# A ViT tower kernel's embedding: both units of every second double group multiplied in rounded parts

## The reference, cut to what matters

```python
xb = 2.0 * jnp.pi * xyz[..., None] * freq_bands            # 6 frequency bands
feat = jnp.concatenate([jnp.sin(xb), jnp.cos(xb)], axis=-1)
feat = feat.reshape(b, n, -1)                              # 4 x 512 x 6912
h = jnp.einsum('bnf,of->bno', feat, W)                     # -> 4 x 512 x 192
```

## Time and profile before

| | value |
|---|---|
| median of 3 runs | 993.34 us (992.94 to 995.34) |
| the profiled execution: its time | 992.54 us |
| its span, first to last instruction | 990.8 us |
| TensorE busy over the span | 896.9 us (91%) |
| VectorE busy over the span | 696.6 us (70%) |
| ScalarE busy over the span | 645.6 us (65%) |
| GpSimd busy over the span | 142.0 us (14%) |
| embedding, first to last matmul | 8.97 us to 288.87 us |
| images 0, 1, 2 (from first matmul to first matmul) | 72.69, 68.62, 68.99 us |

### The profile page before, as it was taken

The page is one execution under the profiler, slowest core; times in us unless marked ns, Lnnn a source line. Parts: engine busy times, 40 slices in busy tenths (PEclk is TensorE's granted clock), DMA queues, the critical chain, the costliest instruction groups (busy, mean ns, idle before and its releaser), DMA issues. The chain is left out here.

```text
span 990.8 us, 19970 instructions
## 1 busy us (share of the span) xinstructions
PE 896.9 (91%) x6459; PEld 794.4 (80%) x6459; DVE 696.6 (70%) x1643; ACT 645.6 (65%) x1218; POOL 142.0 (14%) x204
## 2 busy tenths in 40 slices
PE   6999999999988899989998999898699996699996
PEld 5999999999976677667767776676498875699995
DVE  6889859769633796488648864887556335687775
ACT  5767757649624797589758974987444331886862
POOL 1000000000000144114311441244300000000000
PEclk9999999999997899999999999999789997799997
DMA  8021101089812696169526952795300020443201
GB/s 275 23 71 51 44 27 37 21 125 149 128 34 70 185 293 174 51 210 298 160 58 205 297 156 62 216 294 138 107 1 1 18 87 24 119 164 97 72 2 64
DMA packets 83801, 114.11 MB, mean 115 GB/s; under 512 B 12271, under 2 KB 44476, under 8 KB 83724
## 3 DMA queue, kind: packets, MB, share of 16 engines
q1 hardware_dynamic: 82636, 112.39, 41.2%
q10 hardware_dynamic: 1088, 0.79, 0.2%
HBM read 62.31 MB, written 47.67 MB: 111 GB/s over the span
## 5 line engine op out<-in xcount | busy, mean ns | idle before, releaser
L417 PE MATMUL psum<-w,feat 128*128 128x192 f32 x912 | 160.4, 331 | 11.9 <-ACT feat L347 9.0
L417 PEld LDWEIGHTS psum<-w,feat 128*128 128x128 f32 x912 | 149.3, 192 | 12.8 <-issue 10.3
L646 POOL TENSOR_SCALAR a_scores<-a_scores,a_inv 112x514 f32<-112x514 f32 (+1 forms) x160 | 113.0, 707 | 268.1 <-DVE a_inv L1018 267.9
L1003 DVE CUSTOM_DVE_ANT_0 a_scores<-psum,a_bias 112x514 f32<-112x514 f32 (+1 forms) x160 | 110.0, 688 | 46.6 <-PE psum L722 38.2
L875 ACT ACTIVATE a_scores<-a_scores,a_least 112x514 f32<-112x514 f32 (+1 forms) x160 | 116.7, 729 | 9.8 <-DVE a_least L1003 9.1
L735 PE MATMUL psum<-ident,a_scores 112*112 112x112 f32 (+1 forms) x800 | 100.2, 256 | 18.1 <-DVE a_probsT L1013 10.8
L435 PE MATMUL psum<-w_parts,parts 128*128 128x384 f32 x368 | 113.7, 374 | 0.8 <-DVE parts L227 0.8
L347 ACT ACTIVATE feat<-turn 128x1024 f32<-128x1024 f32 (+1 forms) x60 | 58.4, 974 | 82.5 <-PE psum L437 43.4
L735 PEld LDWEIGHTS psum<-ident,a_scores 112*112 112x112 f32 (+1 forms) x800 | 75.3, 134 | 40.3 <-issue 19.4
L722 PE MATMUL psum<-a_kh,a_q 128*112 128x258 f32 (+1 forms) x320 | 99.6, 333 | 1.0 <-DVE a_least L1003 1.0
L437 PE MATMUL psum<-w_parts,parts 128*128 128x192 f32 x384 | 96.6, 252 | 0.0
(11 more groups left out here) (297 smaller groups left out, 1808.2 us busy)
## 6 DMA issues: line engine op xcount, KB each, us to landing
shear<-a_pos SPq DMA_DIRECT2D x128, 224.9 KB, 3.7
a_bias<-shear SPq DMA_DIRECT2D x128, 224.4 KB, 3.7
shear<-zero SPq DMA_DIRECT2D x20, 448.9 KB, 15.7
e_fc<-in_e_fc_dram SPq DMA_DIRECT2D x16, 384.0 KB, 3.9
x<-in_xT_dram SPq DMA_DIRECT2D x20, 256.0 KB, 3.0
e_proj<-in_e_proj_dram SPq DMA_DIRECT2D x8, 576.0 KB, 5.4
shear<-a_pos SPq DMA_DIRECT2D x32, 130.5 KB
a_bias<-shear SPq DMA_DIRECT2D x32, 130.3 KB
```

The lines of the kernel that those rows point to most:

```text
L417: mm = pe.matmul(sums[m][:, 0:D], feat[:, r, j, 0, 128 * m:128 * m + 128], w[:, k, :], start=begins, stop=ends)
L646: pool.tensor_scalar(row, row, inv[0:TILES[g % NT][1], g % TT:g % TT + 1], 1.0, ALU.mult, ALU.mult).then_inc(weighed, 1)
L1003: dve.tensor_tensor_reduce(halves(scores[0:r, g % TT, 0:PADL]), psum2(score_pair(g), r), halves(bias[0:r, g % MR, :]), -1.0 / 8, BIG, ALU. ...
```

## The change

`full` holds the odd double groups: 1, 3, 5, 7, 9 and 11. Of these the first unit, too, is multiplied in rounded parts; the other groups stay as they were. For each full group and image, ScalarE rounds one more `feat` block (128x1024, both sine and cosine of the unit), VectorE takes one more difference (128x1024), and TensorE runs a second `split` in place of `native`. In the first image there is for each full group one more rounding of weights on ScalarE and one more difference of weights on VectorE. VectorE writes the differences, of both units and of every double group, over the unrounded features in `feat` itself, through a second tensor of type fp32r at the same address (`over`), so that the new array `high` holds only rounded values and has the size of the old `parts`. The raw weights of the full groups arrive by the same transfers as before, into the place in which their difference will stand. The reserved scratch for dynamic DMA is set to 1024 bytes.

```diff
+    full = [g for g in pairs if g % 2 == 1]
+    NFULL = len(full)
+    before = lambda g: sum(e < g for e in full)
+    native_units = [g for g in range(NE) if g not in full]
...
+        def over(n, sh):
+
+            with nc.sbuf_tensor(n, sh, F32) as plain:
+                pass
+            return plain, sb(f"{n}_parts", sh, F32R)
+
         x = sb("x", [128, 5, N])
-        w = sb("w", [128, 2 * NE, D])
+        w_native = sb("w_native", [128, len(native_units), 2, D])
+        w_place, w_first = over("w_first", [128, NFULL, 2, 2, D])
+        first_raw = lambda g: w_place[:, before(g), :, 1, :]
         raw = s.place.rearrange("p (g j n) -> p g j n", g=NPAIR, j=2)
-        feat = sb("feat", [128, NF, 2, 2, N])
+        feat, feat_place = over("feat", [128, NF, 2, 2, N])
         w_parts = sb("w_parts", [128, NPAIR, 2, 2, D], F32R)
-        parts = sb("parts", [128, NF, 2, 2, N], F32R)
+        high = sb("high", [128, NF, 2, 2, N], F32R)
...
-                sp.dma_start(w[:, 2 * g:2 * g + 2, :], s.d["tok_wT"][k0:k0 + 2].rearrange("k p n -> p k n")).then_inc(w_in[g], 16)
+                first = first_raw(g) if g in full else w_native[:, native_units.index(g)]
+                sp.dma_start(first, s.d["tok_wT"][k0:k0 + 2].rearrange("k p n -> p k n")).then_inc(w_in[g], 16)
...
             def rest(b, g):
                 r = g % NF
                 dve.wait_ge(hi_done, b * NPAIR + g + 1)
-                dve.tensor_tensor(parts[:, r, 1], feat[:, r, :, 1, :], parts[:, r, 0].bitcast(F32), ALU.subtract).then_inc(lo_done, 1)
+                dve.tensor_tensor(feat_place[:, r, :, 1, :], feat[:, r, :, 1, :], high[:, r, :, 1, :].bitcast(F32), ALU.subtract).then_inc(lo_done, 1)
+
+            def split_first_weights(g):
+                dve.wait_ge(first_w_hi, before(g) + 1)
+                dve.tensor_tensor(w_first[:, before(g), :, 1, :], first_raw(g), w_first[:, before(g), :, 0, :].bitcast(F32),
+                                  ALU.subtract).then_inc(first_w_lo, 1)
+
+            def first_rest(b, g):
+                r = g % NF
+                dve.wait_ge(first_hi, b * NFULL + before(g) + 1)
+                dve.tensor_tensor(feat_place[:, r, :, 0, :], feat[:, r, :, 0, :], high[:, r, :, 0, :].bitcast(F32), ALU.subtract).then_inc(first_lo, 1)
...
                     absolute(b, g)
+                    if first and g - 1 in full:
+                        split_first_weights(g - 1)
+                    if g - 1 in full:
+                        first_rest(b, g - 1)
                     if g - 1 in pairs:
                         rest(b, g - 1)
...
+            def split_first_weights(g):
+                act.wait_ge(w_in[g], 16)
+                act.copy(w_first[:, before(g), :, 0, :], first_raw(g)).then_inc(first_w_hi, 1)
+
             def first_parts(b, g):
                 r = g % NF
                 act.wait_ge(sin_done, b * NE + g + 1)
                 act.wait_ge(cos_done, b * NE + g + 1)
-                act.copy(parts[:, r, 0], feat[:, r, :, 1, :]).then_inc(hi_done, 1)
+                if g in full:
+                    act.copy(high[:, r, :, 0, :], feat[:, r, :, 0, :]).then_inc(first_hi, 1)
+                act.copy(high[:, r, :, 1, :], feat[:, r, :, 1, :]).then_inc(hi_done, 1)
...
                 group(0, g, True)
+                if g in full:
+                    split_first_weights(g)
                 if g in pairs:
                     split_weights(g)
                     first_parts(0, g)
...
-                def split():
+                def split(unit):
+                    weights = w_parts[:, g] if unit else w_first[:, before(g)]
                     if first:
-                        pe.wait_ge(w_lo, g + 1)
-                    pe.wait_ge(hi_done, b * NPAIR + g + 1)
-                    pe.wait_ge(lo_done, b * NPAIR + g + 1)
+                        pe.wait_ge(*((w_lo, g + 1) if unit else (first_w_lo, before(g) + 1)))
+                    if unit:
+                        pe.wait_ge(hi_done, b * NPAIR + g + 1)
+                        pe.wait_ge(lo_done, b * NPAIR + g + 1)
+                    else:
+                        pe.wait_ge(first_hi, b * NFULL + before(g) + 1)
+                        pe.wait_ge(first_lo, b * NFULL + before(g) + 1)
                     for j in range(2):
+                        both = weights[:, j, :, :].rearrange("p a n -> p (a n)")
                         for m in range(4):
-                            f = lambda part: parts[:, r, part, j, 128 * m:128 * m + 128]
+                            hi = high[:, r, j, unit, 128 * m:128 * m + 128]
+                            lo = feat_place[:, r, j, unit, 128 * m:128 * m + 128]
...
-                                pe.matmul(sums[m][:, 0:2 * D], f(0), w_parts[:, g, j, :, :].rearrange("p a n -> p (a n)"),
-                                          start=False, stop=False)
-                            mm = pe.matmul(sums[m][:, 0:D], f(1), w_parts[:, g, j, 0, :], start=False, stop=False)
+                                pe.matmul(sums[m][:, 0:2 * D], hi, both, start=False, stop=False)
+                            mm = pe.matmul(sums[m][:, 0:D], lo, weights[:, j, 0, :], start=False, stop=False)
                     return mm
 
-                mm = native(0)
-                mm = native(1)
+                if g in full:
+                    split(0)
+                else:
+                    native(0)
+                    mm = native(1)
                 if n == 2:
-                    mm = split()
+                    mm = split(1)
...
-    nc = bacc.Bacc("TRN2", target_bir_lowering=False, num_devices=1)
+    nc = bacc.Bacc("TRN2", target_bir_lowering=False, num_devices=1, dynamic_dma_scratch_size=1024)
```

More of the change, by code:

```diff
@@ L80, in embed_phase @@
     w_hi, w_lo, hi_done, lo_done = sem("w_hi"), sem("w_lo"), sem("hi_done"), sem("feat_lo")
+    first_w_hi, first_w_lo, first_hi, first_lo = sem("first_w_hi"), sem("first_w_lo"), sem("first_hi"), sem("first_lo")
     pairs = [g for g in range(NE) if GROUPS[g][1] == 2]
     NPAIR = len(pairs)
+    full = [g for g in pairs if g % 2 == 1]
+    NFULL = len(full)
+    before = lambda g: sum(e < g for e in full)
+    native_units = [g for g in range(NE) if g not in full]
     sums_done, tokens_done, stated, aggregated = sem("sums_done"), sem("tokens_done"), sem("stated"), sem("aggregated")
@@ L405, in group @@
                 n, r = GROUPS[g][1], g % NF
-                if first:
+                if first and g not in full:
                     pe.wait_ge(w_in[g], 16)
@@ L410, in native @@
                     pe.wait_ge((sin_done, cos_done)[j], b * NE + g + 1)
-                    k = 2 * g + j
+                    k = native_units.index(g)
                     for m in range(4):
@@ L416, in native @@
                             pe.wait_ge(tokens_done, b * 4 - 3 + m)
-                        mm = pe.matmul(sums[m][:, 0:D], feat[:, r, j, 0, 128 * m:128 * m + 128], w[:, k, :],
+                        mm = pe.matmul(sums[m][:, 0:D], feat[:, r, j, 0, 128 * m:128 * m + 128], w_native[:, k, j, :],
                                        start=begins, stop=ends)
@@ L428, in split @@
                     for j in range(2):
+                        both = weights[:, j, :, :].rearrange("p a n -> p (a n)")
                         for m in range(4):
-                            f = lambda part: parts[:, r, part, j, 128 * m:128 * m + 128]
+                            hi = high[:, r, j, unit, 128 * m:128 * m + 128]
+                            lo = feat_place[:, r, j, unit, 128 * m:128 * m + 128]
                             if g == j == 0:
                                 for part in range(2):
-                                    pe.matmul(sums[m][:, part * D:part * D + D], f(0), w_parts[:, g, j, part, :], start=False, stop=False)
+                                    pe.matmul(sums[m][:, part * D:part * D + D], hi, w_parts[:, g, j, part, :], start=False, stop=False)
@@ L467, in last_groups @@
                         for j in range(2):
-                            mm = pe.matmul(sums[m][:, 0:D], feat[:, g % NF, j, 0, 128 * m:128 * m + 128], w[:, 2 * g + j, :],
+                            mm = pe.matmul(sums[m][:, 0:D], feat[:, g % NF, j, 0, 128 * m:128 * m + 128], w_native[:, native_units.index(g), j, :],
                                            start=False, stop=g == NE - 1 and j == 1)
```

## The result

| | before | after |
|---|---|---|
| median of 19 runs each | 991.93 us | 997.55 us |
| ratio after/before, 95% interval | | 1.0067, 1.0043 to 1.009 |
| the profiled execution: its time | 992.54 us | 997.46 us |
| its span | 990.8 us | 995.7 us |
| embedding's first matmul to image 1's first | 72.69 us | 81.34 us |

The kernel became slower by 0.67%. The three runs shown first lay 1.4 us above the median of all 19 of the kernel before. The last line belongs to code that the change doesn't touch; over all kernels of this study it came out between 705.0 and 715.6 us. So the embedding is read from its own rows, as the time from its first matmul, and the ratios of whole executions stand beside it where they were taken. All rows, and all times of a stage, are of one profiled execution of each kernel.

What follows compares the result with a forecast made beforehand. TensorE bounds the embedding, but image 0's VectorE-ScalarE chain, 0.25 us a group behind, takes over. Image 0 +9.6 us, images 1 to 3 -2.1, together +7.5 on the 993.34 median: 1000.9 us, range 994.0 to 1004.0.

Steps and rivals of the forecast that it cites:

- the likeliest case of the forecast: Image 0: VectorE's lateness plus half clock behind group 7's gap lose 9.6 us; later images gain 2.1; +7.5 us, chance 0.52.
- the fourth case: Image 0 loses 7.5 us, but images 1 to 3 gain their full 6.3 us; +1.2, 994.5 us, chance 0.10.
- the case in which the clock stays: Image 0: same VectorE chain, no half clock behind the gap; +7.5 - 2.1 = +5.4 us, 998.7 us, chance 0.23.
- TensorE's saving: On TensorE, each full group takes 4.54 us against 4.89, 0.35 less; 8.4 us over 24 if nothing else limits.
- VectorE's durations: On VectorE, a feature difference written in place and strided still takes 1.22 us, with 0 to 0.1 us more as bounds.
- The turns: VectorE's turns in image 0 alternate 5.04 and 5.68 us, 10.72 a pair, against 9.43 us on TensorE.
- The chain takes the bound over: In image 0, TensorE waits for VectorE's late first differences, 3.9 us before group 7; image 0 loses 7.5 instead of gaining 2.1.
- The wait before group 9: Listed sign in image 0: TensorE waits before group 9, released by VectorE's first difference, forecast at 65.93 us.
- The clock: Behind group 7's gap in image 0, TensorE runs 6.4 us at half clock, losing 3.2 us of work; image 0 loses 9.6.
- Images 1 to 3: Later images: VectorE late only behind the sums, waits before groups 1 and 5; each gains 0.7 us, 2.1 together.
- only TensorE's time changes: Rival: VectorE's first differences come in time everywhere; the kernel gains 8.4 us, 984.9 us, chance 0.07.
- a fall of the clock in the later images: Rival: half clock also behind group 1's wait in later images, 3 x 3.2 us more; 1010.5 us, chance 0.08.

Runs made afterwards that it cites:

- e1: Changed kernel with no full group, leaving only in-place differences, strided layout and smaller scratch; 72.70 us to image 1, ratio 0.9997 to the kernel before.
- e4: Changed kernel plus ten unused matmuls on TensorE before group 7 of image 0; 80.55 us to image 1's first matmul, executed once, no ratio.
- e5: Changed kernel with the class token's square roots before group 12 and TensorE's transposes behind group 13 in image 0; ratio 1.0088 to the kernel before.
- e2: Changed kernel with only group 1 full; 77.17 us to image 1's first matmul, 278.28 to image 3's last three groups, no ratio.
- e9: Changed kernel with image 0's square roots before group 12 and TensorE's transposes behind group 11; 78.31 us to image 1, ratio 1.0074 to the kernel before.
- e6: Changed kernel with the six full groups only in images 1 to 3, their weights split at image 0's end; ratio 1.0005 to the kernel before.
- e7: Like e6 but without group 1: groups 3, 5, 7, 9 and 11 full in images 1 to 3; ratio 0.9969 to the kernel before.
- e8: Changed kernel with the features' first differences on GpSimd instead of VectorE; 86.10 us to image 1's first matmul, ratio 1.0215 to the kernel before.
- e11: Like e7, with groupwise weight splitting in image 0's turns and group 8 full too; ratio 0.996 to the kernel before.
- e12: Like e11, with image 0's square roots before group 12 and transposes behind group 11; median 984.05 us, ratio 0.9933 to the kernel before.

## Why the prediction was right, point by point

By its rows, the likeliest case of the forecast was the one that came, and the time lay in its range. Two terms of the sum were mis-sized, in opposite directions. The whole time alone wouldn't have told the cases apart: 997.55 us lies between the 1000.9 of the forecast and the 994.5 of the fourth case, and nearest to the 998.7 of the case in which the clock stays.

- **TensorE's saving** (forecast 0.35 us for a full group): nearly right. In image 2 groups 8 and 9 take 9.43 us (209.03 - 199.60, the first matmuls of groups 8 and 10), against 9.76 before, so a full group saves 0.33. In image 0 the same two take 71.50 - 61.94 = 9.56 us, 0.20 saved: the pairs of matmuls take 0.29 us there instead of 0.283, the slower pace again. Behind a wait the first row lasts 0.41 us instead of 0.36, so that a full group saves 0.27 there.
- **VectorE's durations:** right. 1.22 us in place, and e1 shows no cost of the writing in place, the strides and the scratch.
- **The turns:** right. 5.06 and 5.67 us for 5.04 and 5.68, the wait moved as described.
- **The chain takes the bound over:** right. The first differences end at 20.35, 42.25, 55.56, 66.02 and 75.41 us (groups 1, 5, 7, 9, 11) for 20.27, 42.17, 55.49, 65.93 and 75.31; the gap before group 7 is 3.66 us for 3.9. The wait before group 9 that the prediction named as a sign did not come. By its own sum it couldn't, with the clock at half: 68.12 is past 65.93.
- **The clock** (forecast 6.4 us at half, 3.2 us of work, 2.1 of which come out in the end): this term was too large. The fall came behind both gaps, but lasted 3.4 us, 1.7 us of work. Group 9 starts at 66.86 instead of 68.12. The sentence quoted from the Trainium skill ("TensorE: Matmul & The Clock Gate", section "What's actually happening"), that activity releases the throttle, agrees with e4, where 3.44 us of other matmuls stood in place of the gap and the clock stayed at 1.00. The step that failed is the one from the earlier trace rows to here: a length of low clock read behind one gap is not the length behind another. The trace of before already had a shorter one, in a later stage:

```profile
536.10:539.30 3.20, 3.20 (x19) 3.15 (x17) 2.45 (x8) 2.94 (x8) 1.26 (x2) 0.50 0.87 269
```

And of the two later falls among the six gaps one came 0.4 us behind its gap, not some microseconds. Behind the gap before group 1, of 2.73 to 2.83 us, the clock was low for 3.4 us in the kernel after, in e4 and in e5, for 6.8 us in e2, and not at all in e9. What decides it stays open, so the fall itself could not be counted on. That a half clock behind group 1 would be taken up was right (e9). Image 0 came to +8.65 us, for +9.6.

- **Images 1 to 3** (forecast -0.7 us each): this term was too large as well. They gave +0.03, -0.50 and -0.57, together -1.04 for -2.1. The mechanism is the one forecast: TensorE waits 1.00, 0.94 and 0.96 us at group 1, and again at group 5. Group 5 starts later than before by 1.27 us in image 1 (116.31 - 90.36 against 106.34 - 81.66) and by 0.84 us in image 2 (184.71 - 159.01 against 175.14 - 150.28), where I had worked out 0.70 from image 2 and taken it for all three. From group 5 on, 1.24 and 1.34 us come back, for 1.40. Most of the miss is thus image 1, which I hadn't worked out by itself. e6 shows that it isn't a rest of image 0's lateness, and e7 that group 1 is what costs. There is more to it. In the kernel before, groups 1 to 6 of images 2 and 3 ran at the slower pace: up to the transposes behind group 6 these images take 34.71 and 34.67 us, and image 1 34.44. In the kernel after none of the three is slow there. So some 0.27 of image 2's 0.50 us and 0.23 of image 3's 0.57 are not the change's; at equal pace the three images give about +0.03, -0.23 and -0.34. The forecast had taken TensorE's start of group 5 from that slower image (24.86 us behind the image's start, for 24.68 in image 1), and so the wait there as too short.
- **The sum:** +7.61 us at the last three groups, for +7.5. The two misses, 1.0 us each, cancel; that agreement is luck. In the profiled execution the rest of the kernel happened to take 2.8 us less, so it shows +4.9 us, 997.46 for 1000.1. The ratio of the 19 runs stands for +4.3 to +8.9 us of 991.93, which holds the 7.6.
- **The chances:** the first, second and last case add up to 0.83, not 0.82, and the case faster had 0.07, not 0.08. Nothing hangs on it.

Of the rivals, that only TensorE's time changes fell with the gaps, that the later images gain all of theirs fell with their 68.65 and 68.49 us, and a fall of the clock in the later images did not come: it is 1.00 in both, with waits of 1 us. That the clock stays fell with the 0.50 in the windows; but image 0's +8.65 lies about halfway between that case (+7.5) and the forecast (+9.6).

## What to carry to other kernels

The bound engine's busy share doesn't tell what happens when work moves from it to a helper; compare the time of one turn of each engine, stage by stage. Here 4.64 us stood beside 4.89, and 1.44 us more for the helper in each pair of turns turned 2.1 us of gain in image 0 into 8.65 us of loss (some 3.0 of them through two table loads in the same chain), while the same change put only where the helper has slack (images 1 to 3, from group 3 on) gains. When a wait or a producer is moved, follow it to the other engine's queue at the end of the stage too: in e5 a copy of 0.15 us held VectorE for 4.40 us.

## What the runs showed of the hardware beyond that

- TensorE's clock at half lasted either 3.4 or 6.8 us in the embeddings of these kernels: 3.4 us behind gaps of 2.73 and 3.66 us (after), 2.81 (e4), 2.83 (e5) and 2.03 us (e8, twice); 6.8 us with gaps of 2.83 (e2), 5.87 (e5), 3.70 and 4.81 us (e8), where it fell 0.4 us or more before the gap's end. Behind one gap of 2.83 us (e9) and one of 2.03 (e8, image 3) it stayed at 1.00, and so it did behind the waits of about 1 us in images 1 to 3. What decides between these is open. Ten matmuls without use, in place of the 3.66 us gap, shortened image 0 by 0.79 us.
- The same code ran at two paces with the clock at 1.00 in both: eight pairs of rounded matmuls in 2.27 or 2.32 us (e7 and e11), image 3 in 60.99 or 61.46 us.
- The idle time that the profile shows before a row can be less than the wait: 0.49 and 0.28 us for two waits that cost 1.24 us together (before and e12).
- GpSimd and VectorE on 128x1024 fp32 at once: GpSimd 2.90 us in one case, 3.59 us on average and 6.59 us at most in image 0, and a VectorE instruction of 0.75 us took 2.85 us (e8).
